# Layer 2's neighbour weights as 32x32 products in half steps, and layer 1 taken chunk by chunk on two banks

## The chip, the cores and the metric

One core of one Trainium2 chip runs the whole program as one launch. The metric is device time in microseconds: the time from the start to the end of an execution, median of several runs. Five engines work side by side, each through its own instruction queue in order, and meet at semaphores: PE (TensorE, matmul, with its weight loads PEld), DVE (VectorE), ACT (ScalarE), POOL (GpSimd) and SP (SyncE, which here only issues DMAs).

## The reference, cut to what matters

Four graph layers follow one another on 2048 nodes with 64 features each, x of 2048x64 and adj of 2048x2048 with entries 0 or 1. After each layer the input is added and the row is normalised.

```python
# layer 0
deg = max(sum(adj, axis=1) + 1, 1)
z = concat([X, (adj @ X + X) / deg]) @ W + b;  out = relu(z) / |relu(z)|
# layer 1
u = tanh([X, t] @ W1 + b1) @ W2 + b2;  XB = X @ B.T
out = u + adj @ XB - sum(adj, axis=1) * XB
# layer 2: weights halve from each neighbour to the one before it
rank = cumsum(adj != 0, axis=1);  deg = rank[:, -1];  k = min(deg, 100)
pos = rank - (deg - k);  w = (adj != 0) * where(pos > 0, 0.5 ** (k - pos), 0)
out = w @ (input @ weight) + bias
# layer 3
s = adj @ (tanh(|x|) * x / |x|);  out = (arctanh(|s|) * s / |s|) @ kernel + bias
```

So four products with a 2048x2048 matrix are made, three with adj and one with w. For a neighbour in w only the number of later neighbours in its row counts: each of them halves its weight.

## The kernel before, in words

The 2048 nodes (columns of the transposed matrix) are cut into 4 chunks `e` of 512 and into 16 blocks `c` of 128. The adjacency comes in 16 loads of 128 rows (`load_lower` on SP, `load_upper` on ACT). DVE turns each load with two 32x32 stream transposes into bf16 (`transposes`, L550 to L557), into `AT[:, c, e]`, 128 partitions by 512 columns per block and chunk. All four layers' sums over neighbours then are 16 matmuls per chunk of 128x128 by 128x512 (`sum_block`, L801), `XP` (x in two fp16 parts) standing and the matrix moving.

Per chunk of layer 0, PE counts each row's neighbours by quarter (`counts`, L845, products with 32 output rows, four of them side by side in the array), ACT copies the counts to `cnt` (`take_counts`, L381), PE makes the degrees from them (`degrees`, L875), and DVE takes these (`take_degrees`). PE sums (L801) and adds the own row (`add_own`), ACT takes the sum (`take_sum`, L391), PE multiplies with the layer's weights (`dense`, L934), POOL scales the own part by the degree (`weigh`, L276), and DVE finishes the chunk: `activate0`, `combine0`, `normalise`, the last of which ends with two instructions (L561, L562) that write the parts XP of layer 1. Layer 1 needs all four chunks' parts for every sum. It also needs `transpose_x` (L827), `take_xt`, `hidden` (L903) and `take_hidden`, each of which uses the one bank psX in turn.

Layer 2's weights are made beside layers 0 and 1. A bf16's bits, read as int16, grow by 128 where the number doubles. So PE forms, in fp32, 12800 where there is a neighbour, less 128 for each later neighbour, and ACT writes it with a Relu as int16 into `WT`, where it is read as the bf16 weight. Before, this is a running sum, the "chain": two sums that stay in two banks, each going down eight blocks of a chunk, 64 blocks in all. A block is two products of 128x128 by 128x512,

```python
nc.tensor.matmul(acc, C("past"), AT[:, c + 1, e], start=False, stop=False, ...)   # L890
nc.tensor.matmul(acc, C("own"), AT[:, c, e], start=False, stop=True, ...)         # L892
```

and one eviction of 128x512 (`take_chain`, L397); block n waits until the eviction of block n-2 has freed its bank. The order of the whole is written out by hand, engine by engine: where the 64 blocks stand among the sums is in `CHAIN_IN_SUMS` and at the end of the PE program (L945 to L1053). 38 of the 64 blocks stand ahead of the last chunk's counts, 8 more up to the last parts of layer 1, and 18 behind.

Line numbers are those of the kernel before; the changed kernel's differ.

## Time and profile before

| | |
|---|---|
| median of 3 runs | 167.0 us (166.5 to 167.3) |
| profiled execution, own time | 167.19 us |
| profiled execution, span of the instructions | 165.3 us |
| busy: PE, PEld | 123.7 us (75%), 67.6 us |
| busy: DVE, ACT, POOL | 105.8 us (64%), 70.6 us, 46.3 us |

The page cuts the span into 40 slices of 4.1 us and gives each engine's busy share in tenths:

```profile
PE   0000269996999999999997999989999899992000
DVE  0164997999999999998961115500623888538861
ACT  0030215477567866715814576721113310257440
PEclk9999999999999999999999999999999999998555
```

The row PEclk is the clock that TensorE was granted, in tenths of its upper level. Rows of a timeline give start and duration in microseconds from the start of the span; `x16` means 16 instructions in one row; `[1.06 <-DVE AT L557]` is idle time of the engine ahead of the row and the instruction that ended it. Products overlap in the array, so the distance of two starts is what a product costs PE, and its duration is how long until its result is there.

### The profile page before, as it was taken

How to read it: one execution, taken by the hardware profiler on the slowest of the kernel's cores; microseconds unless marked ns; L12 is line 12 of the kernel's file. 1: busy time of each engine (PE TensorE's matmuls, PEld its weight loads, DVE VectorE, ACT ScalarE, POOL GpSimd, SP SyncE). 2: the span in 40 equal slices, each digit the busy share in tenths (PEclk: the TensorE clock that was granted, in tenths of full speed). 3: DMA queues.
4: the chain of work that ended last, by engine and by line, in shares of the span. 5: the costliest groups of instructions: out<-in, count | busy, mean ns of one | idle time of the engine just before them, and what ended most of it. 6: DMA issues, size and time to landing. Idle time of an engine off the chain costs nothing.

```text
span 165.3 us, 2143 instructions
## 1 busy us (share of the span) xinstructions
PE 123.7 (75%) x760; PEld 67.6 (41%) x760; DVE 105.8 (64%) x235; ACT 70.6 (43%) x143; POOL 46.3 (28%) x54
## 2 busy tenths in 40 slices
PE   0000269996999999999997999989999899992000
PEld 0000159841444345346344667337447644572000
DVE  0164997999999999998961115500623888538861
ACT  0030215477567866715814576721113310257440
POOL 0000002412401241027931024400412552713290
PEclk9999999999999999999999999999999999998555
DMA  3999999999999940000000000000000000000006
GB/s 110 255 238 357 354 289 252 337 344 340 339 345 346 300 147 0 0 4 0 0 0 0 0 4 0 2 0 4 0 0 0 0 2 0 4 0 0 0 0 127
DMA packets 13946, 18.59 MB, mean 112 GB/s; under 512 B 5360, under 2 KB 5616, under 8 KB 13936
## 3 DMA queue, kind: packets, MB, share of 16 engines
q1 hardware_dynamic: 7728, 9.68, 20.6%
q10 hardware_dynamic: 6208, 8.78, 18.0%
q8 instruction: 6, 0.10, 0.2%
q14 instruction: 4, 0.03, 0.1%
HBM read 17.93 MB, written 0.52 MB: 112 GB/s over the span
## 4 chain that ended last, share of the span: by engine, by line
DVE 34%; PE 34%; DMA 13%; ACT 5%; POOL 4%; issue 4%; SPq 2%; POOLq 1%; DVEq 0%
PE psS L801 11%; DVE AT L556 8%; DMA stage<-adj 7%; DMA WT<-adj 7%; DVE AT L557 6%; PE psN L801 5%; PE psC L801 5%; POOL root L287 2%; PE psC L892 2%; PE psC L890 2%; POOL nroot L306 2%; DVE XP L562 2%; ACT WT L397 2%; DVE XP L561 1%; DVE u L579 1%
## 5 line engine op out<-in xcount | busy, mean ns | idle before, releaser
L397 ACT ACTIVATE WT<-psC 128x512 int16<-128x512 f32 x64 | 36.5, 597 | 13.3 <-PE psC L892 12.4
L801 PE MATMUL psS<-AT,XP 128*128 128x512 bf16 x112 | 29.9, 379 | 1.3 <-DVE XP L562 1.3
L287 POOL TENSOR_TENSOR root<-var,power 128x4 f32<-128x4 f32 (+1 forms) x16 | 18.7, 1172 | 36.5 <-DVE var L603 14.6
L892 PE MATMUL psC<-AT,cb 128*128 128x512 bf16 x64 | 24.2, 379 | 0.0
L890 PE MATMUL psC<-AT,cb 128*128 128x512 bf16 x56 | 21.4, 382 | 1.6 <-ACT WT L397 1.5
L556 DVE STREAM_TRANSPOSE AT<-stage 128x1024 bf16<-128x1024 bf16 x10 | 13.0, 1304 | 10.0 <-DMA stage<-adj 10.0
L801 PEld LDWEIGHTS psS<-AT,XP 128*128 128x128 f16 x112 | 10.4, 98 | 15.1 <-DVE XP L562 2.3
L854 PE MATMUL psH<-AT,cb 128*32 128x256 bf16 x32 | 1.7, 344 | 18.9 <-DVE AT L557 18.9
L300 POOL TENSOR_TENSOR XB<-X,weights 128x256 f32<-128x256 f32 x12 | 10.0, 843 | 18.4 <-DVE X L608 18.4
L557 DVE STREAM_TRANSPOSE AT<-stage 128x1024 bf16<-128x1024 bf16 x10 | 12.7, 1273 | 0.0
L391 ACT ACTIVATE stage<-psS 128x512 f32<-128x512 f32 x6 | 3.6, 596 | 17.6 <-PE psS L801 11.4
L890 PEld LDWEIGHTS psC<-AT,cb 128*128 128x128 bf16 x56 | 5.8, 103 | 12.1 <-ACT WT L397 9.1
L619 DVE TENSOR_TENSOR t<-psH,XB 128x256 f32<-128x256 f32 x3 | 1.3, 425 | 14.1 <-PE psH L937 13.1
L619 DVE TENSOR_TENSOR t<-psN,XB 128x256 f32<-128x256 f32 x3 | 1.3, 424 | 12.8 <-PE psN L937 8.4
L801 PE MATMUL psN<-AT,XP 128*128 128x512 bf16 x32 | 9.2, 379 | 0.0
L608 DVE TENSOR_TENSOR X<-t,root 128x256 f32<-128x256 f32 x16 | 7.3, 479 | 2.9 <-POOL root L287 2.8
L556 DVE STREAM_TRANSPOSE AT<-WT 128x1024 bf16<-128x1024 bf16 x6 | 8.0, 1328 | 1.6 <-DMA WT<-adj 1.6
L854 PEld LDWEIGHTS psH<-AT,cb 128*32 128x32 bf16 x32 | 0.9, 111 | 19.0 <-issue 18.9
L281 POOL TENSOR_TENSOR ssroot<-ss,power 128x4 f32<-128x4 f32 x4 | 4.1, 1023 | 15.5 <-DVE ss L581 15.3
L801 PE MATMUL psC<-AT,XP 128*128 128x512 bf16 x32 | 7.7, 379 | 0.8 <-ACT WT L397 0.8
L412 ACT ACTIVATE v<-t 128x256 f32<-128x256 f32 x12 | 4.9, 421 | 7.7 <-DVE t L619 6.7
L801 PE MATMUL psS<-WT,XP 128*128 128x512 bf16 x32 | 7.9, 379 | 0.0
(156 smaller groups left out, 231.1 us busy)
## 6 DMA issues: line engine op xcount, KB each, us to landing
stage<-adj ACTq DMA_DIRECT2D x20, 256.0 KB, 11.3
stage<-adj SPq DMA_DIRECT2D x20, 256.0 KB, 13.4
WT<-adj ACTq DMA_DIRECT2D x12, 256.0 KB, 12.5
WT<-adj SPq DMA_DIRECT2D x12, 256.0 KB, 16.8
out<-X SPq DMA_DIRECT2D x6, 64.0 KB, 2.0
weights<-weights_packed SPq DMA_DIRECT2D x1, 353.5 KB, 17.2
X<-x SPq DMA_DIRECT2D x2, 128.0 KB, 6.8
X<-x ACTq DMA_DIRECT2D x2, 128.0 KB, 8.2
```

The costliest lines, as they stand in the source:

```text
L281: nc.gpsimd.tensor_tensor(ssroot[:, chunk(e)], ss[:, chunk(e)], power[:, 0, 0:NR], ALU.pow).then_inc(ssroot_ready, 1)
L287: nc.gpsimd.tensor_tensor(root[:, e, 0:n], var[:, e, 0:n], power[:, 0:n, 0:NR], ALU.pow).then_inc(root_ready, 1)
L300: nc.gpsimd.tensor_tensor(XB[:, chunk(e)], X[:, chunk(e)], per_feature(W(f"b{l}")), ALU.add).then_inc(xb_ready, 1)
L391: nc.scalar.activation(to.rearrange("p (k h b) -> p k h b", h=2, b=QD), natural(sum_bank(l, e)[:]), ACT.Copy, scale=scale).then_inc(sum_ta ...
L397: nc.scalar.activation(WT[:, e, chain_block(bank, k)], psC[bank][:], ACT.Relu).then_inc(chain_taken, 1)
L412: nc.scalar.activation(v[:, chunk(e), 0:D], t[:, chunk(e)], ACT.Square, scale=0.125).then_inc(square_ready, 1)
L556: nc.vector.transpose(to[:, :, :, :, 0], halves[:, :, 0, :, :, 1])
L557: nc.vector.transpose(to[:, :, :, :, 1], halves[:, :, 1, :, :, 1]).then_inc(transposed, 1)
L608: nc.vector.tensor_tensor(X[:, chunk(e)], t[:, chunk(e)], per_node(root[:, e, 0]), ALU.mult).then_inc(x_ready, 1)
L801: ins = nc.tensor.matmul(bank, XP[:, l % 2, c], matrix, start=(c == 0), stop=last)
L890: nc.tensor.matmul(acc, C("past"), AT[:, c + 1, e], start=False, stop=False, skip_group_check=True)
L892: nc.tensor.matmul(acc, C("own"), AT[:, c, e], start=False, stop=True, skip_group_check=(k > 0)).then_inc(chain_ready, 1)
```

## The change

**The chain.** The 64 blocks become 16 steps of four blocks. psC is now four banks, one for each quarter (32 partitions of the block). In a step, quarter q of block g gets two products of 32x32 by 32x512: one of the table `base` with `later` (the counts of all later blocks and quarters, so no running sum is left), and one of `own` with 32 partitions of AT. A half step is two quarters: 8 products of the first kind and 8 of the second, in two banks; ACT evicts both banks at once (128x1024). The half step waits until its own two banks are free. `later` comes from a new product (`spread`) and a new eviction (`take_spread`), once per chunk, between the counts and the degrees; degrees now wait for it.

**Order within layer 2.** WT now holds the nodes in another order. So layer 2's parts are written to ZP, turned by 16 products per chunk (`turn`), and evicted to XP (`take_turned`).

**Layer 1.** Its four sums had banks of their own and ran side by side; now they use two (psN, psS), chunk by chunk. The counts of chunks 1 to 3 go to psX, which transpose_x and hidden use too. Of the last chunk, the counts and sums of 384 columns are made as soon as 15 of the 16 transposes are done, the rest after the sixteenth.

**The rest.** The centring of the weights goes from DVE's end of layer 0 to its fourth transpose, `weights` is loaded one load earlier, `activate0` keeps its rows in `v`, and its first instruction is a step of its own (`add_own_part`). POOL forms the residuals of chunks 0 and 1 right after their diagonals.

Around the counts of the last chunk PE had this order before (psX: the bank of transposes and hidden products; L845 are the counts):

```order
L827 MATMUL psX<-cb,XP 128x128 x4
L890 MATMUL psC<-AT,cb 128x512
L892 MATMUL psC<-AT,cb 128x512
L890 MATMUL psC<-AT,cb 128x512
L892 MATMUL psC<-AT,cb 128x512
L903 MATMUL psX<-stage,weights 128x512
L845 MATMUL psH<-AT,cb 32x512 x16
L801 MATMUL psS<-AT,XP 128x512 x8
L875 MATMUL psH<-cb,cnt 128x1 x4
L801 MATMUL psS<-AT,XP 128x512 x8
```

and has this one now (L968 is the dense product, L852 the transpose, L940 hidden, L872 the counts, L915 and L920 a half step):

```order
L968 MATMUL psH<-weights,sum 128x64 x4
L852 MATMUL psX<-cb,XP 128x128 x4
L940 MATMUL psX<-stage,weights 128x512
L852 MATMUL psX<-cb,XP 128x128 x4
L915 MATMUL psC<-later,cb 32x512 x8
L920 MATMUL psC<-AT,cb 32x512 x8
L915 MATMUL psC<-later,cb 32x512 x8
L920 MATMUL psC<-AT,cb 32x512 x8
L940 MATMUL psX<-stage,weights 128x512
L872 MATMUL psX<-AT,cb 32x384 x16
```

Two transposes and two hidden products, where there was one of each, now stand ahead of the last counts, and the counts wait for the second `take_hidden`. ACT's queue at the same place before, from the chain's evictions of chunk 2 to the counts:

```order
L375 ACTIVATE stage<-psX 128x512
L397 ACTIVATE WT<-psC 128x512 x2
L408 ACTIVATE stage<-psX,weights 128x512
L381 ACTIVATE cnt<-psH 128x512
L391 ACTIVATE sum<-psS,xs 128x512
```

and now:

```order
L395 ACTIVATE sum<-psS,xs 128x512
L402 ACTIVATE WT<-psC 128x1024
L375 ACTIVATE stage<-psX 128x512
L418 ACTIVATE stage<-psX,weights 128x512
L375 ACTIVATE stage<-psX 128x512
L402 ACTIVATE WT<-psC 128x1024 x2
L418 ACTIVATE stage<-psX,weights 128x512
L380 ACTIVATE cnt<-psX 128x512
```

Here too a second pair of take_xt (L375) and take_hidden (L418) has come in, and the two evictions of a chain step (L402) stand between them.

The diff, cut to its core:

```diff
-CCOLS = {"ident": P, "paired": P, "own": P, "past": P, "begin0": P, "begin1": P, "count": QD, "each": 1}
+NBLOCKS = 16
+CCOLS = {"ident": P, "paired": P, "own": QD, "base": NBLOCKS * QD, "spread": P, "count": NQ * QD, "each": 1}
...
-        psS = [psum(f"psS{i}", [P, CW], F32) for i in range(2)]
-        psC = [psum(f"psC{i}", [P, CW], F32) for i in range(2)]
-        psN = [psum(f"psN{i}", [P, CW], F32) for i in range(2)]
+        ZP = Z[:].rearrange("p c f -> p (c f)").bitcast(F16).rearrange("p (c f) -> p c f", c=NB)
+
+        psC = psum("psC", [P, NQ, CW], F32)
+        psS = psum("psS", [P, CW], F32)
+        psN = psum("psN", [P, CW], F32)
...
         def sum_bank(l, e):
-            return psS[0] if l == 0 else (psS[1], psN[1], psS[0], psC[0])[e]
+            if l == 0:
+                return psS[:]
+            return (psN[:], psS[:])[e % 2] if l == 1 else (psN[:], psC[:, 2], psC[:, 3], psS[:])[e]
 
         def z_bank(e):
-            return (psN[0], psN[1], psS[1], psC[0])[e]
+            return (psN[:], psC[:, 1], psC[:, 2], psC[:, 3])[e]
 
         def dense_bank(l, e):
-            return psN[0] if l == 0 else (psN[0], psH)[e % 2] if l == 1 else (psN[0], psH, psX, psC[1])[e]
-
-        CHAIN_IN_SUMS = (0, 10, 27, 38)
-        CHAIN_LOOP = 46
-        CHAIN_ALL = NB * NE
-
-        def chain_in_sums(e):
-            return range(CHAIN_IN_SUMS[e], min(CHAIN_IN_SUMS[e] + NB // 2, NB * e))
-
-        def chain_after_sums(e):
-            return range(chain_in_sums(e).stop, CHAIN_IN_SUMS[e + 1])
+            if l == 0:
+                return psH[:]
+            return (psH[:], psH[:], psX[:], psH[:])[e] if l == 1 else (psH[:], psX[:], psC[:, 0], psC[:, 1])[e]
+
+        def turn_bank(e):
+            return psC[:, e % 2]
...
                 diagonals(e)
-            e = NE - 2
-            weigh(e)
-            l2_root(e)
-            weigh(e + 1)
-            residual(1, 0)
-            var_root(0, e)
-            diagonals(e)
-            residual(1, 1)
-            l2_root(e + 1)
-            diagonals(e + 1)
+                residual(1, e)
+            weigh(2)
+            diagonals(2)
+            l2_root(2)
+            weigh(3)
+            l2_root(3)
+            var_root(0, 2)
+            var_root(0, 3)
+            diagonals(3)
...
+            def take_spread(e):
+                act.wait_ge(spread_ready, e + 1)
+                nc.scalar.activation(natural(later[:, e % 2]), psX[:].rearrange("p (k h b) -> p k h b", h=2, b=QD),
+                                     ACT.Copy).then_inc(spread_taken, 1)
...
-            def take_chain(n):
-                act.wait_ge(chain_ready, n + 1)
-                e, k, bank = n // NB, n % NB // 2, n % 2
-                nc.scalar.activation(WT[:, e, chain_block(bank, k)], psC[bank][:], ACT.Relu
+            def take_chain(i, h):
+                act.wait_ge(chain_ready, PAIRS * i + h + 1)
+                e, m = i // NR, i % NR
+                tiles = slice(NQ * m + PAIRS * h, NQ * m + PAIRS * (h + 1))
+                nc.scalar.activation(WT[:, e, tiles], psC[:, PAIRS * h:PAIRS * (h + 1)], ACT.Relu
                                      ).then_inc(chain_taken, 1)
 
-            def take_pair(n):
-                take_chain(n)
-                take_chain(n + 1)
+            def take_step(i):
+                for h in range(PAIRS):
+                    take_chain(i, h)
+
+            def take_turned(e):
+                act.wait_ge(turned, e + 1)
+                nc.scalar.activation(XP[:, 0, chunk(e)], turn_bank(e).rearrange("p (Q f) -> p Q f", Q=NQ),
+                                     ACT.Copy).then_inc(turned_taken, 1)
...
+            take_step(7)
+            take_spread(2)
+            take_chain(8, 0)
+            take_sum(0, 2)
+            take_chain(8, 1)
+            take_xt(1, 0)
+            take_hidden(0)
+            take_xt(1, 1)
+            take_step(9)
+            take_hidden(1)
+            take_counts(3)
+            take_sum(0, 3)
+            take_spread(3)
+            take_step(10)
...
-                parts = XP[:, l % 2, chunk(e)]
+                parts = ZP[:, chunk(e)] if l == 2 else XP[:, l % 2, chunk(e)]
...
             transposes(14)
+            add_own_part(2)
             transposes(15)
             activate0(2)
-            bundle = W(CENTRED[0], CENTRED[-1]).rearrange("p (k f) -> p k f", f=D)
-            step(nc.vector.tensor_reduce(wmean[:], bundle, AX_X, ALU.add))
-            nc.vector.scalar_tensor_tensor(bundle, wmean[:].unsqueeze(2).to_broadcast([P, len(CENTRED), D]), -1.0 / D,
-                                           bundle, ALU.mult, ALU.add).then_inc(centred, 1)
             take_degrees(3)
+            add_own_part(3)
+            activate0(3)
             combine0(2)
-            activate0(3)
+            combine0(3)
             normalise(0, 2)
-            combine0(3)
             normalise(0, 3)
...
+            def counts(e, cols=slice(0, CW)):
+                if e == NE - 1:
+                    pe.wait_ge(hid_taken, 2)
+                bank = psH if e == 0 else psX
...
+            def spread(e):
+                pe.wait_ge(counts_taken, e + 1)
+                nc.tensor.matmul(psX[:], C("spread"), cnt[:].rearrange("p r Q b -> p (r Q b)"), start=True, stop=True
+                                 ).then_inc(spread_ready, 1)
+
             def degrees(e):
-                pe.wait_ge(counts_taken, e + 1)
+                pe.wait_ge(spread_taken, e + 1)
                 for r in range(NR):
                     c = NR * e + r
-                    ins = nc.tensor.matmul(psH[:, c:c + 1], cnt[:, e % 2, r].rearrange("p Q b -> p (Q b)"),
+                    ins = nc.tensor.matmul(psX[:, c:c + 1], cnt[:, r].rearrange("p Q b -> p (Q b)"),
                                            C("each"), start=True, stop=True)
                 ins.then_inc(deg_ready, 1)
 
-            def chain(n):
-                e, k, bank = n // NB, n % NB // 2, n % 2
-                acc, c = psC[bank][:], chain_block(bank, k)
-                if n == 0:
+            def chain(i):
+                e, m = i // NR, i % NR
+                if i == 0:
                     pe.wait_ge(z_taken, NE)
-                if n >= 2:
-                    pe.wait_ge(chain_taken, n - 1)
-                if k == 0:
-                    nc.tensor.matmul(acc, C(f"begin{bank}"), cnt[:, e % 2].rearrange("p r (k h) b -> p (r k) b h", h=2),
-                                     start=True, stop=False)
-                else:
-                    nc.tensor.matmul(acc, C("past"), AT[:, c + 1, e], start=False, stop=False,
-                                     skip_group_check=True)
-                nc.tensor.matmul(acc, C("own"), AT[:, c, e], start=False, stop=True,
-                                 skip_group_check=(k > 0)).then_inc(chain_ready, 1)
-
-            def chain_pair(n):
-                chain(n)
-                chain(n + 1)
+                if m == 0:
+                    pe.wait_ge(spread_taken, e + 1)
+                for h in range(PAIRS):
+                    if i >= 1:
+                        pe.wait_ge(chain_taken, PAIRS * (i - 1) + h + 1)
+                    for q in range(PAIRS * h, PAIRS * (h + 1)):
+                        rows = slice(QD * q, QD * (q + 1))
+                        for g in range(NQ):
+                            c = NQ * m + g
+                            nc.tensor.matmul(psC[QD * g:QD * (g + 1), q], C("base")[rows, QD * c:QD * (c + 1)],
+                                             later[rows, e % 2], start=True, stop=False)
+                    for q in range(PAIRS * h, PAIRS * (h + 1)):
+                        rows = slice(QD * q, QD * (q + 1))
+                        for g in range(NQ):
+                            ins = nc.tensor.matmul(psC[QD * g:QD * (g + 1), q], C("own")[rows],
+                                                   AT[rows, NQ * m + g, e], start=False, stop=True)
+                    ins.then_inc(chain_ready, 1)
+
+            def turn(e):
+                pe.wait_ge(parts_ready, parts_count(2, e))
+                pe.wait_ge(chain_taken, PAIRS * STEPS)
+                if e >= 2:
+                    pe.wait_ge(turned_taken, e - 1)
+                for q in range(NQ):
+                    for g in range(NQ):
+                        ins = nc.tensor.matmul(turn_bank(e)[QD * g:QD * (g + 1), P * q:P * (q + 1)],
+                                               C("ident")[:, QD * q:QD * (q + 1)], ZP[:, NQ * e + g],
+                                               start=True, stop=True)
+                ins.then_inc(turned, 1)
...
+            for e in range(1, NE - 1):
+                pe.wait_ge(transposed, NR * (e + 1))
+                pe.wait_ge(deg_taken, e)
+                counts(e)
+                for c in range(NB):
+                    sum_block(0, e, c)
+                    if c == 1:
+                        chain(NR * e - 1)
+                    if c == 5:
+                        spread(e)
+                    if c == 10:
+                        degrees(e)
+                    if c == 11:
+                        chain(NR * e)
+                add_own(0, e)
+                sums(1, 0, range(e - 1, e))
+                dense(0, e)
...
+            pe.wait_ge(transposed, NB - 1)
+            counts(e, most)
+            pe.wait_ge(sum_taken, e)
+            sum_cols(e, 0, 3)
             pe.wait_ge(transposed, NB)
+            counts(e, rest)
+            sum_cols(e, 3, 4)
+            chain(10)
+            spread(e)
             degrees(e)
+            dense(0, e)
+            sums(1, 1, range(0, 1))
+            chain(11)
+            sums(1, 1, range(1, 2))
+            chain(12)
+            transpose_x(1, 2)
+            sums(1, 0, range(2, 3))
+            hidden(2)
+            sums(1, 1, range(2, 3))
+            chain(13)
             sums(1, 0, late)
             add_own(1, 0)
+            transpose_x(1, 3)
             sums(1, 1, late)
             add_own(1, 1)
+            hidden(3)
             dense(1, 0)
+            chain(14)
+            sums(1, 2, every)
             add_own(1, 2)
             dense(1, 1)
+            chain(15)
+            sums(1, 3, every)
+            add_own(1, 3)
             dense(1, 2)
+            turn(0)
+            turn(1)
             dense(1, 3)
+            for g in range(2):
+                for e in every:
+                    sums(2, e, range(g, g + 1))
+            turn(2)
+            turn(3)
```

## Rows read from the trace of the kernel before

**Rows 1.** Windows, us from the start of the span: busy time of each engine and granted clock.
```profile
core 0: us, PE busy (x) PEld busy (x) DVE busy (x) ACT busy (x) POOL busy (x), PEclk, DMA share, GB/s
...
69.90:87.70 17.80, 16.55 (x99) 7.93 (x100) 15.32 (x35) 7.26 (x13) 10.14 (x11) 1.00 0.00 1
87.70:112.10 24.40, 23.18 (x140) 13.47 (x141) 5.28 (x12) 14.29 (x28) 4.72 (x5) 1.00 0.00 1
...
149.80:151.90 2.10, 0.02 (x1) 0.00 (x0) 1.83 (x10) 1.13 (x6) 0.00 (x0) 1.00 0.00 0
151.90:165.30 13.40, 0.00 (x0) 0.00 (x0) 7.54 (x30) 5.00 (x22) 5.64 (x5) 0.50 0.19 39
```

**Rows 2.** Timeline of PE, 41 to 57 us: start, duration, instructions, [idle before <-releaser].
```profile
41.38 1.05 PE L845 MATMUL psH<-AT,cb 128*32 128x512 bf16 x16 [1.06 <-DVE AT L557]
42.35 0.61 PE L801 MATMUL psS<-AT,XP 128*128 128x512 bf16 x2
...
56.98 1.05 PE L845 MATMUL psH<-AT,cb 128*32 128x512 bf16 x16
```

**Rows 3.** Groups of instructions on ACT: count, busy us, mean ns, idle before.
```profile
L397 ACT ACTIVATE WT<-psC 128x512 int16<-128x512 f32 x64 | 36.5, 597 | 13.3 <-PE psC L892 12.4
...
L364 ACT ACTIVATE Z<-psN 128x256 f32<-128x256 f32 x2 | 0.8, 384 | 0.4 <-PE psN L836 0.4
```

**Rows 4.** Timeline of ACT: one pair of the chain's evictions.
```profile
37.23 1.09 ACT L397 ACTIVATE WT<-psC 128x512 int16<-128x512 f32 x2 [0.21 <-PE psC L892]
```

**Rows 5.** Timeline of DVE, chunk 0 of layer 0, 36 to 47 us.
```profile
36.60 0.29 DVE L578 TENSOR_SCALAR y<-t 128x256 f32<-128x256 f32 x1
...
38.83 1.33 DVE L556 STREAM_TRANSPOSE AT<-WT 128x1024 bf16<-128x1024 bf16 x1
...
41.23 0.38 DVE L589 TENSOR_TENSOR t<-y,ssroot 128x256 f32<-128x256 f32 x1
...
43.09 1.31 DVE L556 STREAM_TRANSPOSE AT<-stage 128x1024 bf16<-128x1024 bf16 x1
...
45.48 0.38 DVE L608 TENSOR_TENSOR X<-t,root 128x256 f32<-128x256 f32 x1
...
46.22 0.43 DVE L562 SCALAR_TENSOR_TENSOR XP<-X,XP 128x256 f16<-128x256 f32 x1
46.56 1.32 DVE L556 STREAM_TRANSPOSE AT<-stage 128x1024 bf16<-128x1024 bf16 x1
```

**Rows 6.** Timeline of DVE, chunk 3 of layer 0, 73 to 88 us.
```profile
73.58 0.15 DVE L568 TENSOR_SCALAR degp<-psH 128x4 f32<-128x4 f32 x1
...
77.06 0.42 DVE L576 TENSOR_TENSOR t<-psN,Z 128x256 f32<-128x256 f32 x1 [0.32 <-PE psN L934]
...
86.77 0.83 DVE L562 SCALAR_TENSOR_TENSOR XP<-X,XP 128x256 f16<-128x256 f32 x1
```

**Rows 7.** Timeline of POOL, 74 to 88 us.
```profile
74.21 0.72 POOL L276 TENSOR_TENSOR Z<-Z,degp 128x256 f32<-128x256 f32 x1 [1.56 <-DVE ndeg L570]
...
86.49 0.83 POOL L300 TENSOR_TENSOR XB<-X,weights 128x256 f32<-128x256 f32 x1 [0.54 <-DVE X L608]
```

**Rows 8.** Timeline of PE, 69 to 121 us.
```profile
69.89 1.05 PE L845 MATMUL psH<-AT,cb 128*32 128x512 bf16 x16 [0.36 <-DVE AT L557]
...
79.60 1.02 PE L903 MATMUL psX<-stage,weights 128*128 128x512 f32 x2
80.46 0.38 PE L890 MATMUL psC<-AT,cb 128*128 128x512 bf16 x1
...
92.33 0.33 PE L936 MATMUL psN<-weights,stage 128*128 128x64 f32 x2
...
94.06 0.38 PE L890 MATMUL psC<-AT,cb 128*128 128x512 bf16 x1
...
120.74 1.89 PE L801 MATMUL psS<-WT,XP 128*128 128x512 bf16 x8
```

358 lines of the change are left out of this document (154 added, 204 removed).

## The prediction, made before the changed kernel was run

> **What bounds the kernel now.** I read the page's slices first, then windows, then the timelines of PE, ACT, DVE and POOL from 40 to 132 us. The slices show two regimes: to about 70 us DVE is full (the 16 transposes and layer 0 between them), from there PE is, until 150. The windows say the same in numbers: after the last chunk's counts begin, PE is busy 16.55 of 17.80 us, then 23.18 of 24.40 [rows 1]. Between the two lies one path: the counts of the last chunk start at 69.89 [rows 8], DVE takes the degrees at 73.58, the dense product at 77.06, and writes layer 1's last parts up to 86.77 + 0.83 = 87.60 [rows 6]. In those 17.8 us PE lives on blocks of the chain. Whoever makes the chain cheap frees PE, but the path has to become shorter too, or PE waits.
>
> The profiled execution took 167.19 us for a span of 165.3; the median of the runs is 167.0. I work out a shift of the span and add it to 167.0. Less than 0.5% (0.84 us) can't be told from no change.
>
> **Prices.** Eight sums of 512 columns last 1.89 us, the last one 0.38 of it, so one costs PE (1.89 - 0.38)/7 = 0.216, and its result comes 0.17 later [rows 8]. The 16 products of the counts, four at a time in the array, cost 42.35 - 41.38 = 0.97 us [rows 2]: four rounds of 0.216, and 0.10 for the change of tiling. So column tiles run fully side by side. No row shows row tiles. If they did nothing, a step's 32 products would be 8 rounds, 1.73 us, as much as the eight products of four blocks now (8 x 0.216). If all 16 tiles ran freely it would be 2 rounds, 0.43. I take 3 rounds, since the second product of a half must wait for the first on its own tiles while the next half can start beside it: 0.65, and with two changes of tiling 0.85. I take it nearer the fast end, because the nearest row, the counts, shows no loss at all from sharing the array.
>
> The page "TensorE: Matmul & The Clock Gate" of the Trainium skill (Measured speedup vs the span model) gives 10.6x for 16 tiles of 32x32. That lies near the fast end; no row here shows it, and by it a step would be some 0.2 us shorter than mine.
>
> An eviction of 512 columns takes 597 ns, one of 256 takes 384 [rows 3], so 1024 columns are 597 + 512 x 0.83 = 1.02 us. A second one behind the first costs 1.09 - 0.60 = 0.49 [rows 4], so one of 1024 costs 0.49 + 0.43 = 0.92. ACT then needs 1.84 us a step; now it spends 1.09 + 0.21 on a pair of blocks, 2.6 on four [rows 4]. On ACT the chain falls from 64 x 0.49 = 31 us to 16 x 1.84 = 29, with 8 new evictions of 0.6: nothing won.
>
> **The change up to the last chunk's counts.** Taken from PE here: 38 blocks of 0.43; added: 10 steps of 0.85. None of it shows while DVE is full. DVE pays a little: residual(1, 0) now runs on POOL while DVE writes chunk 0's parts, and one DVE instruction beside such a POOL instruction takes 0.83 [rows 6, 7] against 0.43 [rows 5], so 0.4. The centring (1.2 us) falls into DVE's wait for the fifth load, which I book at 0.3, with `weights` ahead of a load; between 0 and 1. So the counts of chunk 2 start at 56.98 + 0.7 = 57.7 [rows 2].
>
> From there everything stands in one line, since psX is passed from hand to hand. Chunk 2: counts 0.97, 16 sums 3.45, spread, degrees and own row 0.55, steps 7 and 8 1.7, result 0.2: 64.6. take_sum 0.6 and dense 0.85 (16 fp32 products cost 94.06 - 92.33 = 1.73, eight of them half [rows 8]): 66.1. Transpose 0.4, eviction 0.6, hidden 0.86 + 0.17 (80.46 - 79.60 [rows 8]), eviction 0.6: 68.7. Transpose 0.4 and eviction 0.6: 69.7. The second hidden product is made under step 9, but ACT has the step's two evictions in front of take_hidden, 1.9 + 0.6: 72.2. Only then is psX free for the last counts. Before, they started at 69.89, as soon as DVE was done; that early start of three quarters of them, which the change provides, is lost in this queue.
>
> **From the counts to layer 1's last parts.** Counts and sums of 384 columns 0.75 + 2.6 + 0.2; the rest 0.3 + 0.1 + 0.9 + 0.1; step 10 0.85; spread 0.4, its eviction 0.6, degrees 0.3: 7.1, so 79.3, against 73.58 [rows 6]. DVE has stood still since 73 and holds combine0(2) behind take_degrees(3). Then degrees 0.5, weigh 0.7 [rows 7], the own part 0.4, activate0 38.83 - 36.60 = 2.2, two combine0 of 43.09 - 41.23 = 1.86, normalise(0, 2) 46.56 - 45.48 = 1.1 [rows 5]: 87.9. normalise(0, 3) 1.1 + 0.4 (a diagonal on POOL beside it): 89.4, against 87.6. PE runs out of work at about 84.5 and waits until 87.9.
>
> **Layer 1 and the start of layer 2.** From 87.9: transpose, 8 sums, hidden, step 13: 3.6. Then 8 sums 1.7, own rows 0.4, transpose and hidden 1.1, waits for take_hidden(2) and take_xt, which stand behind evictions of step 13, 1.1. Four dense products 6.9, steps 14 and 15 1.7, 32 sums 6.9, own rows 0.4, two turns 0.6 (16 products of 128 columns are four rounds of 0.056). That ends at 112.3. Half of layer 2's sums 6.9: 119.2. The last two turns and the wait for their eviction (0.1 + 0.22 + 0.2 + 0.6 + 0.1): 120.4, or 120.7 with a DVE step of `activate0` now writing rows of 65 elements (up to 0.13 four times). Before, the same sums start at 120.74 [rows 8]. From here nothing changes but banks, 0 to 0.2. So PE's saving (26 blocks of 0.43 = 11 us less 6 steps of 0.85 = 5) is eaten by the later parts, 1.8, by 20 more sums behind them, 4.3, less what lies ahead of the last parts, by turns of 1.5 and by waits. The waits for ACT in layer 1 and DVE's cost ahead of chunk 2 are unsure by 0.4 each, and the bounds put both on top: shift 0 to +0.8, taken as +0.4: **167.4 us**.
>
> **Rivals.**
>
> *The path is shorter than I reckon (faster).* If the hand-overs on psX overlap more, or ACT reaches take_hidden(1) ahead of step 9's evictions, the last counts start with DVE's end, 2.5 us earlier, and with them the parts. PE has the spare time for it: it stands 3.4 us in my account. 167.4 - 2.5 = 164.9, down to 162 if DVE never waits. For it speaks the 6 us less of work on PE, and that a stage whose engine is full at 93% gains from less work; against it, that each link of the path has a row of its own.
>
> *The clock falls (slower).* PE's clock stayed full from 25.6 to 149.8 us, in which its longest pause was 1.06 us [rows 2], and was at 0.50 from 151.9, 2.1 us after its last product [rows 1]. The change brings pauses: about 3 us ahead of chunk 1's counts, 3.5 ahead of chunk 2's, 3.4 before 87.9. If the clock is at 1.2 GHz after one of them, PE-bound work runs at half speed until it comes back; at the start it took from 21.9 to 25.6, so 3.7 us at half speed, 1.85 lost. The place is 87.9 us, where every us counts: 169.3; with a second fall at 57.7, 171.1. It decides as soon as a pause of 2 us or more comes in mid-kernel. Against it: the one fall seen came after a stretch of fp32 products, and a pause in mid-kernel of this length is in no row.
>
> The same page of the Trainium skill (HAM oscillation) warns of just this, pauses between bursts of products that bring the clock back down; the only pause of that kind in this trace, the end, agrees with it.
>
> *Row tiles don't run side by side (slower; the change then doesn't do what it says).* A step costs 1.08 more. Of the 16, steps 7, 8, 10, 13, 14 and 15 lie on my path: +6.5, less 1 that ACT's pace hides: 173.
>
> **Chances.** My own account, within 1.2 us of 167.4: 0.38, of which 0.22 is no change and 0.16 slower. Faster by the shorter path: 0.30. The clock: 0.22. Row tiles: 0.10. Faster 0.30, same 0.22, slower 0.48. The range takes in the clock's double fall and leaves out row tiles and the lowest of the fast cases: 164.3 to 171.1.
>
> **What would show it.** Right: starts of L915 and L920 within a half in groups of eight, a step's first start to the next PE instruction 0.75 to 0.95; last counts (L872, 32x384) at 71 to 73; a DVE pause of 5 us or more ended by degrees; a PE pause of 3 us before the transpose of chunk 2; layer 2's third group of sums at 120 to 122. Wrong: the last counts ahead of 70, or PE without a pause between 80 and 88 (then faster); groups of four (row tiles); a PEclk under 1.00 between 26 and 150 us.

## The result and the profile after

| | before | after |
|---|---|---|
| median | 167.0 us (166.5 to 167.3, 4 runs) | 173.4 us (172.8 to 173.9, 4 runs) |
| ratio | | 1.038, 95% interval 1.034 to 1.043 |
| span of the profiled execution, its own time | 165.3, 167.19 us | 172.0, 173.86 us |
| busy: PE, PEld | 123.7, 67.6 us | 113.2, 63.2 us |
| busy: DVE, ACT, POOL | 105.8, 70.6, 46.3 us | 106.2, 70.5, 46.2 us |

The change made the kernel 3.8% slower, and the time lies above my range of 164.3 to 171.1. PE's busy time is 10.5 us lower and the span 6.7 us longer. (The trace of the changed kernel has lost some records of products: the page counts 1230 beside 1244 weight loads. Run 1 below has them all; less its 52 extra products of 0.216 us its busy time is 110.5 us, so at full clock PE does 13 us less than before.) The slices of the changed kernel:

```profile
PE   0000289970986499669735979999989989994000
...
PEclk9999999995699569999995799999999999999555
```

Two things are new. PE has holes in the slices that begin at 38.7, 55.9 and 86.0 us (each is 4.3 us). And PEclk is low in three places in mid-kernel, where before it was full. The windows of the changed kernel give the clock its bounds (columns as in [rows 1]):

```profile
core 0: us, PE busy (x) PEld busy (x) DVE busy (x) ACT busy (x) POOL busy (x), PEclk, DMA share, GB/s
...
39.10:45.90 6.80, 2.88 (x37) 0.80 (x50) 6.56 (x13) 1.98 (x3) 2.40 (x3) 0.50 1.06 340
45.90:56.20 10.30, 8.33 (x162) 3.65 (x131) 9.96 (x19) 7.59 (x9) 2.90 (x4) 1.00 1.06 339
56.20:63.00 6.80, 4.31 (x61) 0.96 (x53) 6.66 (x10) 2.39 (x4) 2.26 (x3) 0.50 0.67 194
...
90.30:97.10 6.80, 4.79 (x13) 2.11 (x14) 4.51 (x9) 0.60 (x1) 3.75 (x5) 0.50 0.00 0
```

At 0.50 the clock is at the lower of its two levels, 1.2 instead of 2.4 GHz ("half clock" below). PE's timeline shows what it did before each fall. The longest idle time in mid-kernel before the change was 1.06 us [rows 2]:

```profile
35.19 0.41 PE L915 MATMUL psC<-later,cb 32*32 32x512 bf16 x8
...
37.93 0.41 PE L915 MATMUL psC<-later,cb 32*32 32x512 bf16 x8 [0.29 <-ACT WT L402]
38.15 0.40 PE L920 MATMUL psC<-AT,cb 32*32 32x512 bf16 x8
42.69 1.90 PE L872 MATMUL psX<-AT,cb 128*32 128x512 bf16 x16 [4.14 <-DVE AT L573]
```

```profile
54.88 0.41 PE L915 MATMUL psC<-later,cb 32*32 32x512 bf16 x8 [1.10 <-ACT WT L402]
...
56.02 0.53 PE L920 MATMUL psC<-AT,cb 32*32 32x512 bf16 x8
58.71 1.90 PE L872 MATMUL psX<-AT,cb 128*32 128x512 bf16 x16 [2.16 <-DVE AT L573]
```

```profile
87.72 0.40 PE L920 MATMUL psC<-AT,cb 32*32 32x512 bf16 x8
92.31 0.58 PE L852 MATMUL psX<-cb,XP 128*128 128x128 bf16 x4 [4.19 <-DVE XP L578]
```

The first fall, at 39.1, came 0.55 us after PE's last product, and ahead of that PE had made a half step every 0.92 us. The second, at 56.2, came in the half step at 56.02, after a pause of 1.10; the pause of 2.16 came only then. The third, at 90.3, came some 2.2 us into a pause of 4.19. The 16 counts then took 1.90 us, against 1.05 at full clock [rows 2, 8].

The milestones of the path, in the order of the prediction (start of the PE row, where no other is named; the last column is the run with extra products that follows):

| | before | predicted | after | after, clock kept full |
|---|---|---|---|---|
| counts, chunk 1 | 41.38 | | 42.69 | 42.65 |
| counts, chunk 2 | 56.98 | 57.7 | 58.71 | 57.90 |
| counts, chunk 3 | 69.89 | 72.2 | 75.96 | 73.44 |
| DVE takes its degrees | 73.58 | 79.3 | 83.17 | 80.65 |
| PE goes on with chunk 2's parts | | 87.9 | 92.31 | 89.79 |
| last parts written (DVE) | 87.60 | 89.4 | 95.12 | 92.61 |
| layer 2, third group of sums | 120.74 | 120.4 to 120.7 | 127.68 (see below) | 122.67 |

The row at 127.68 holds 7 of the 8 products of its group, so the group will have started one product earlier, at about 127.46. From the third group on both kernels take the same, 44.6 and 44.5 us to the end of the span. DVE's timeline around the last chunk shows the other half of the loss, the wait for the degrees, with work for chunk 2 standing behind them:

```profile
75.17 0.43 DVE L603 SCALAR_TENSOR_TENSOR v<-ymean,v 128x256 f32<-128x256 f32 x1
83.17 0.16 DVE L584 TENSOR_SCALAR degp<-psX 128x4 f32<-128x4 f32 x1 [7.58 <-PE psX L898]
...
91.73 0.43 DVE L578 SCALAR_TENSOR_TENSOR XP<-X,XP 128x256 f16<-128x256 f32 x1
92.27 1.26 DVE L627 TENSOR_TENSOR X<-t,root 128x256 f32<-128x256 f32 x1
...
94.29 0.83 DVE L578 SCALAR_TENSOR_TENSOR XP<-X,XP 128x256 f16<-128x256 f32 x1
```

And PE's, ahead of the last counts, the hand-overs on psX. For the idle 0.82 us the profile names no releaser; `transpose_x(1, 1)` waits there for the first `take_hidden`, which runs on ACT from 71.50 to 72.19:

```profile
69.27 0.39 PE L852 MATMUL psX<-cb,XP 128*128 128x128 bf16 x4
70.34 1.12 PE L940 MATMUL psX<-stage,weights 128*128 128x512 f32 x2 [0.69 <-ACT stage L375]
72.29 0.38 PE L852 MATMUL psX<-cb,XP 128*128 128x128 bf16 x4 [0.82 <-issue]
...
73.36 1.12 PE L940 MATMUL psX<-stage,weights 128*128 128x512 f32 x2
75.96 0.83 PE L872 MATMUL psX<-AT,cb 128*32 128x384 bf16 x16 [1.47 <-ACT stage L418]
```

### The profile page after: what moved, and what is told of

It is laid out like the page before. It is cut to its first block, busy times and chain, and to the rows that moved or that the text cites. A ratio compares the mean times of both kernels' runs of the same rounds, so it can differ in the third digit from the quotient of the medians.

```text
span 172.0 us, 3082 instructions
## 1 busy us (share of the span) xinstructions
PE 113.2 (66%) x1230; PEld 63.2 (37%) x1244; DVE 106.2 (62%) x235; ACT 70.5 (41%) x119; POOL 46.2 (27%) x54
## 4 chain that ended last, share of the span: by engine, by line
PE 37%; DVE 29%; DMA 10%; ACT 8%; issue 4%; POOL 4%; SPq 4%; POOLq 1%; another core or an unknown queue 0%; DVEq 0%
DMA stage<-adj 10%; PE psN L823 7%; PE psC L823 7%; PE psS L823 6%; DVE AT L573 6%; DVE AT L572 6%; ACT WT L402 3%; PE psX L940 2%; PE psS L880 2%; SPq L246 2%; POOL nroot L308 2%; PE psX L872 2%; PE psH L970 2%; PE psH L971 2%; POOL root L289 2%
## 5 line engine op out<-in xcount | busy, mean ns | idle before, releaser
L402 ACT ACTIVATE WT<-psC 128x1024 int16<-128x1024 f32 x32 | 31.1, 1022 | 15.5 <-PE psC L920 14.8
L823 PE MATMUL psS<-AT,XP 128*128 128x512 bf16 x74 | 20.5, 397 | 1.2 <-issue 1.1
L872 PE MATMUL psH<-AT,cb 128*32 128x256 bf16 x32 | 1.7, 343 | 19.1 <-DVE AT L573 19.1
L823 PEld LDWEIGHTS psS<-AT,XP 128*128 128x128 f16 x80 | 7.4, 102 | 12.8 <-issue 6.3
L915 PE MATMUL psC<-later,cb 32*32 32x512 bf16 x256 | 9.2, 409 | 2.7 <-ACT WT L402 2.7
L627 DVE TENSOR_TENSOR X<-t,root 128x256 f32<-128x256 f32 x16 | 8.1, 534 | 4.1 <-POOL root L289 4.0
L872 PE MATMUL psX<-AT,cb 128*32 128x512 bf16 (+2 forms) x64 | 5.0, 451 | 7.8 <-DVE AT L573 6.3
L880 PE MATMUL psS<-AT,XP 128*128 128x256 bf16 (+2 forms) x64 | 9.3, 304 | 0.2 <-ACT cnt L380 0.2
L920 PE MATMUL psC<-AT,cb 32*32 32x512 bf16 x256 | 9.0, 394 | 0.0
L852 PE MATMUL psX<-cb,XP 128*128 128x128 bf16 x32 | 3.5, 240 | 7.5 <-DVE XP L578 4.2
L872 PEld LDWEIGHTS psH<-AT,cb 128*32 128x32 bf16 x32 | 0.9, 111 | 19.2 <-issue 19.1
L572 DVE STREAM_TRANSPOSE AT<-WT 128x1024 bf16<-128x1024 bf16 x6 | 7.9, 1312 | 0.0
L573 DVE STREAM_TRANSPOSE AT<-WT 128x1024 bf16<-128x1024 bf16 x6 | 7.7, 1279 | 0.0
L823 PE MATMUL psC<-WT,XP 128*128 128x512 bf16 x32 | 7.6, 379 | 0.0
```

Of the source, the lines that this page charges most:

```text
L402: nc.scalar.activation(WT[:, e, tiles], psC[:, PAIRS * h:PAIRS * (h + 1)], ACT.Relu).then_inc(chain_taken, 1)
L572: nc.vector.transpose(to[:, :, :, :, 0], halves[:, :, 0, :, :, 1])
L573: nc.vector.transpose(to[:, :, :, :, 1], halves[:, :, 1, :, :, 1]).then_inc(transposed, 1)
L627: nc.vector.tensor_tensor(X[:, chunk(e)], t[:, chunk(e)], per_node(root[:, e, 0]), ALU.mult).then_inc(x_ready, 1)
L823: ins = nc.tensor.matmul(sum_bank(l, e), XP[:, l % 2, c], matrix, start=(c == 0), stop=last)
L872: ins = nc.tensor.matmul(bank[QD * g:QD * (g + 1), cols], one, AT[:, NQ * g + k, e, cols], start=(k == 0), stop=(k == NR - 1))
```

## The experiments

The kernel before ran beside each group of runs, at 166.9 to 167.1 us. Theory at this point: of the 6.4 us, the clock's three falls are some 4 and the path to layer 1's parts the rest. The rival: the falls cost nothing, since they lie in pauses, and all is path. Where milestones of two runs are compared below, note that the loads alone move them: chunk 2's counts start at 58.13 us in run 8 and at 57.24 in run 11, which differ only behind them.

**1. The clock kept full.** Products whose result nobody reads fill PE's pauses; the kernel's own waits stay, and one is added so that the bank of the last group is free. 52 of them, of 512 columns, stand around steps 1 and 2, 5 and 6, and 12:

```diff
+            def keep_busy(bank, n):
+                for _ in range(n):
+                    nc.tensor.matmul(bank, C("ident"), AT[:, 0, 0], start=True, stop=True)
...
+            keep_busy(psN[:], 1)
             chain(1)
+            keep_busy(psN[:], 1)
             chain(2)
+            keep_busy(psN[:], 17)
...
                     chain(NR * e + 1)
+                    keep_busy(psS[:], 4)
                     chain(NR * e + 2)
+                    keep_busy(psS[:], 8)
...
+            pe.wait_ge(dense_taken, NE)
+            keep_busy(psH[:], 4)
             chain(12)
+            keep_busy(psH[:], 17)
```

> The changed kernel with extra products of 128x128 by 128x512 on PE, whose results nobody reads, in the three places where its clock fell: between and behind chain steps 1 and 2 (19), behind steps 5 and 6 (12), around step 12 (21). Theory A (the clock is what I missed): PEclk stays 1.00 in all three places; the 1.9 us that chunk 2 of layer 0 took longer at the lower clock and the 2.5 us of the stretch behind 92.3 us come back: 169.0 us, 168.2 to 170. Theory B (the path through the counts and DVE is what costs, the clock falls where PE waits anyway): within 1 us of 173.4.

Measured: 169.4 us (169.0 to 169.7), ratio to before 1.0146 (1.012 to 1.018). The page's row of the clock is full up to the end, and the last counts start at 73.44:

```profile
PEclk9999999999999999999999999999999999999655
```

```profile
38.88 3.84 PE L981 MATMUL psN<-AT,cb 128*128 128x512 bf16 x17
42.65 1.05 PE L872 MATMUL psX<-AT,cb 128*32 128x512 bf16 x16
```

```profile
73.44 0.83 PE L872 MATMUL psX<-AT,cb 128*32 128x384 bf16 x16 [1.47 <-ACT stage L418]
...
89.79 0.38 PE L852 MATMUL psX<-cb,XP 128*128 128x128 bf16 x4 [0.42 <-DVE XP L578]
```

PE has more to do and the kernel is 4.0 us faster. (Chunk 1's counts stand behind the 17 products, 38.88 + 3.84, so they gain nothing here.) So the three falls cost 4.0 us, though each begins in or beside a pause: what costs is that the half clock reaches into the work behind it. The two traces say where: of the changed kernel's delay 0.8 us stand at chunk 2's counts, 1.7 more at the last counts, none up to chunk 2's parts, and 2.3 between these and layer 2's third group (4.8; the two profiled executions themselves differ by 4.9, 173.86 and 169.0). The rest, 169.4 against 167.0, is path.

**2. Only the last fall prevented** (the seven lines around step 12 alone: 4 products, 17 products and the wait).

> The same extra products around step 12 alone, so the clock falls only twice. Theory A: the third fall costs 2.5 us, all of it on the path: 170.9 us, and the first two falls stay where they were. Theory B: within 0.7 us of 173.4.

Measured: 171.5 us (169.9 to 172.3), ratio 1.025 (1.018 to 1.033). Two early stretches at half clock stayed (38.3 to 48.6 and 58.8 to 62.2), none late. So by the medians the late one is worth some 1.9 us, the early two together 2.1; the runs spread over 2.4 us, so the split is unsure by about 1. The traces above gave 2.3 and 2.5.

**3. DVE's order around the last degrees.** Chunk 2 is finished before the last degrees are awaited, as it was not in the change:

```diff
             activate0(2)
+            combine0(2)
+            normalise(0, 2)
             take_degrees(3)
             add_own_part(3)
             activate0(3)
-            combine0(2)
             combine0(3)
-            normalise(0, 2)
             normalise(0, 3)
```

and on POOL `var_root(0, 2)` stands ahead of `weigh(3)`.

> The changed kernel with combine0(2) and normalise(0, 2) ahead of take_degrees(3) on DVE (and chunk 2's root ahead of weigh(3) on POOL), in DVE's pause of 7.6 us. If DVE's queue behind the degrees is on the path: 3.0 us less, and since the transpose, hidden product and sums of chunk 2 then fill PE's pause before 92 us, the third fall of the clock should go as well: 168 us, 167 to 169.5. If only the last counts' own time matters (PE-bound behind it): 1 us or less.

Measured: 167.7 us (167.3 to 168.4, 10 runs), ratio 1.005 (1.003 to 1.007). DVE's wait for the degrees shrank from 7.58 us to 2.77, and chunk 2's transpose on PE had no pause ahead of it, so the third stretch at half clock was gone as well:

```profile
79.57 0.42 DVE L578 SCALAR_TENSOR_TENSOR XP<-X,XP 128x256 f16<-128x256 f32 x1
82.76 0.16 DVE L584 TENSOR_SCALAR degp<-psX 128x4 f32<-128x4 f32 x1 [2.77 <-PE psX L898]
```

```profile
87.71 0.40 PE L852 MATMUL psX<-cb,XP 128*128 128x128 bf16 x4
...
93.14 1.04 PE L823 MATMUL psN<-AT,XP 128*128 128x512 bf16 x4 [1.04 <-DVE XP L578]
```

This one order is worth 5.7 us, the largest single part. By run 2 some 1.9 of it is the third fall. Against run 2 itself, where the late clock is full as well, it is 3.8 us, but not all of that is the wait for the degrees: the last counts, ahead of everything the order touches, start at 75.62 here and at 76.12 in run 2, with the early stretches at half clock shorter (6.8 and 3.4 us, against 10.2 and 3.4). That leaves some 3.3 for the wait itself.

**4. The centring put back** behind DVE's last transposes, with the residuals of chunks 0 and 1 behind `l2_root(2)` on POOL and the load of the weights one load later:

```diff
+            transposes(4)
+            transposes(5)
             dve.wait_ge(weights_loaded, 16)
...
-            bundle = W(CENTRED[0], CENTRED[-1]).rearrange("p (k f) -> p k f", f=D)
...
-            transposes(4)
-            transposes(5)
             take_degrees(0)
...
             activate0(2)
+            bundle = W(CENTRED[0], CENTRED[-1]).rearrange("p (k f) -> p k f", f=D)
...
             take_degrees(3)
```

> The changed kernel with the centring back behind activate0(2), the load of the weights back behind the fourth load, and residual(1, 0) and (1, 1) on POOL behind l2_root(2). If DVE's early part is what moved the first two chunks: counts of chunk 1 at 41.4 instead of 42.7, of chunk 2 at 57.0 instead of 58.7, and 1.7 us less: 171.7 us. If the later waits absorb it: within 0.7 us of 173.4.

Measured: 172.5 us (172.0 to 172.9), ratio 1.033 (1.030 to 1.036): 0.9 us, between the two. Chunk 1's counts start at 42.39, 0.3 earlier, and chunk 2's at 58.73, no earlier than in the change. DVE waits for chunk 0's degrees, which in the profiled execution of the change were there without a wait:

```profile
32.92 0.17 DVE L720 SCALAR_TENSOR_TENSOR weights<-weights 128x1 f32<-128x1 f32 x1
34.34 0.16 DVE L585 TENSOR_SCALAR degp<-psX 128x4 f32<-128x4 f32 x1 [1.25 <-PE psX L899]
```

The degrees stand behind `spread` and its eviction now: from chunk 0's second counts to the degrees PE takes 2.85 us here (31.20 to 34.05), 1.62 in the kernel before. That wait is not the centring's doing alone. With the centring early, as in the change, DVE still waited 1.26, 0.63 and 1.11 us in runs 2, 3 and 5, and took the degrees at 34.73, 34.49 and 34.38, against 34.34 here: wherever the centring stands, they come at the same time. As in run 3, though, the second stretch at half clock was 3.4 us long and the last counts start 0.4 earlier (75.57), near half of the 0.9.

**5. Second transpose and hidden product behind the last counts**, so that only one pair passes psX ahead of them:

```diff
                     transpose_x(1, 0)
                     hidden(0)
-                    transpose_x(1, 1)
                     chain(NR * e + 1)
-                    hidden(1)
...
             chain(11)
+            transpose_x(1, 1)
             sums(1, 1, range(1, 2))
+            hidden(1)
             chain(12)
```

with ACT's `take_xt(1, 1)` and `take_hidden(1)` behind step 11.

> The changed kernel with transpose_x(1, 1), hidden(1) and their two evictions behind the last chunk's degrees, between steps 11 and 12, so that the last counts wait for the first take_hidden alone. Theory A (the hand-over of psX in front of the last counts is on the path): the last counts start near 73 instead of 75.96 us and 3 us go: 170.4 us, 169.5 to 171.3. Theory B (what is moved comes back behind the parts, where PE is full): within 0.8 us of 173.4.

Its four runs gave 169.1 us three times and 166.4 once, and only one of the 169.1 was profiled. So this run gives no firm size: the gain is 4.3 us by three of the runs and 7.0 by the fourth, of which no trace exists. In the trace that there is, the last counts start at 71.98 instead of 75.96 and the pause before chunk 2's parts shrank to 2.60 us, and the third stretch at half clock with it (88.9 to 92.4); with the second stretch, 3.4 us here too, that is why it is more than expected.

**6. The chain at near its old price.** Every half step makes its 16 products twice.

```diff
                 for h in range(PAIRS):
                     if i >= 1:
                         pe.wait_ge(chain_taken, PAIRS * (i - 1) + h + 1)
+                    for _ in range(2):
...
```

> The changed kernel with the 16 products of every half step made twice, so that a step costs PE 8 rounds, as much as the four blocks before; nothing else changes. It asks what the cheap chain is worth in this order. If PE's work counts where the steps lie on the path (7, 8, 10, 13 to 15): 5 us more, 178. If the chain was hidden and the clock is what matters, less pausing pays back: 171 to 174.

Measured: 178.4 us (177.6 to 180.1), ratio 1.065 (1.061 to 1.069). The last counts start at 79.19. So the cheap products do shorten the path, by 5.0 us in this order, although the denser PE also had less of the half clock (13.7 us in three stretches, against 20.5 in the change). And since the doubled kernel stands 11.4 us above the kernel before, what surrounds the products, the clock's falls with it, loses at least that much. A doubled step is still cheaper than four blocks were: two quarters' second pass runs beside the other half's first. PE's rows of run 10, which has the same steps, show it:

```profile
62.21 0.41 PE L917 MATMUL psC<-later,cb 32*32 32x512 bf16 x8
62.44 0.40 PE L922 MATMUL psC<-AT,cb 32*32 32x512 bf16 x8
62.62 0.44 PE L917 MATMUL psC<-later,cb 32*32 32x512 bf16 x16
62.84 0.44 PE L922 MATMUL psC<-AT,cb 32*32 32x512 bf16 x16
63.05 0.44 PE L917 MATMUL psC<-later,cb 32*32 32x512 bf16 x8
63.27 0.46 PE L922 MATMUL psC<-AT,cb 32*32 32x512 bf16 x8
63.66 1.04 PE L824 MATMUL psS<-AT,XP 128*128 128x512 bf16 x4
```

It takes 63.66 - 62.21 = 1.45 us, a single step at this place 0.61 (below), four blocks before 1.73.

**7. The three orders together** (runs 3, 4 and 5).

> DVE's order of e3_dve_order, the centring back as in e4_centring_back, and the late hidden product of e6_hidden_late together. If the three act on the same path one after the other: 167.7 less 3 less 0.9, so 163.8 us, 162.5 to 165.5, faster than the kernel before (167.0). If PE is full behind the last parts by then and only the front moves: 166 to 167.5.

Measured: 166.4 us (165.4 to 167.5, 12 runs), ratio 0.997 (0.994 to 0.999). The second reading holds; the gains are not a sum. The clock was still at half from 40.0 to 46.8 and from 57.1 to 63.9.

**8. The same with the first two places filled** (18 products around steps 1 and 2, 12 around steps 5 and 6; none late, since no pause is left there).

> The same with the extra products of e1_warm_all behind chunks 0 and 1 (18 and 12), not around step 12. By the clock theory the two falls before 60 us go and 1.5 to 2 us with them against e8_all_orders: 162 us. If DVE's queue sets the pace there: within 0.5 us of e8_all_orders.

Measured: 164.1 us (163.6 to 164.6, 6 runs), ratio 0.982 (0.979 to 0.985). It is 2.9 us below the kernel before. PEclk is full from start to end of the products:

```profile
PEclk9999999999999999999999999999999999999555
```

**9. Run 8 with the centring where the change put it.**

> As the run with all three orders and the early extra products (164.1 us), but the centring and the residuals stand where the change put them. Putting them back was worth 0.9 us in the changed kernel as it is. Theory A (what precedes chunk 2's counts is on the path, whatever the clock): slower by about 0.9, so 165.0. Rival (the 0.9 came with the places of the clock's falls, which are gone here): 164.1 within 0.3.

Measured: 164.1 us (163.3 to 164.6), ratio 0.983 (0.978 to 0.987). The rival holds: in run 8 DVE waited 1.31 us for chunk 0's degrees, here it does the centring in that time, and the counts of chunk 2 start at 57.94, against 58.13. The centring's place is worth nothing by itself.

**10. Run 8 with the chain doubled, as in run 6.**

> As the run with all three orders and the early extra products (164.1 us), with each half step's 16 products made twice, so that a block costs PE about what it cost before the change. It asks what the cheap products are worth where neither the clock nor the queues cost anything. In the changed kernel doubling cost 5.0 us. Theory A (PE's work from chunk 2's counts on lies on the path; ten of the 16 steps are made behind chunk 2's counts, 0.43 us more each): +4 to +5, so 168 to 169, above the kernel before. Rival (with the queues in order DVE sets the end of layer 0, and only the six steps behind it count): +2.5, so 166.6.

Measured: 172.7 us (172.0 to 173.4), ratio 1.034 (1.030 to 1.039). That is 8.6 us above run 8; both theories were too low. Chunk 2's counts start 2.6 us later (60.70 against 58.13), the last counts 4.3 (74.38 against 70.04), the third group of layer 2's sums 8.1 (126.24 against 118.14). My expectation took 0.43 us for a second pass, and ten steps behind chunk 2's counts. There are nine (7 to 15), and a second pass costs 1.45 - 0.61 = 0.84 us; so they bring up to 7.6, and most of PE's work there is on the path (8.1 - 2.6 = 5.5). Of the 2.6 ahead of it some are loads: DVE waited for them for 1.90, 0.55 and 1.16 us, against 1.14 and 0.28 in run 8. Why they came later was not tried. This run has nearly the old price of the chain, the clock full and the queues in order, and is still 5.6 us above the kernel before. What of this is due to spread, to the turning, to layer 1 on two banks or to the rest, no run separates.

**11. Run 8 with both hidden products ahead of the last counts, as in the change.**

> As the run with all three orders and the early extra products (164.1 us), but the second transpose and hidden product stand ahead of the last chunk's counts, as in the change. Theory A (psX's hand-over is on the path to the last counts): last counts near 72 instead of 70.04, time 165 to 166. Rival (with the clock full the hand-over fits beside DVE's work): 164.1 within 0.3.

Measured: 164.9 us (164.3 to 166.1, 7 runs), ratio 0.988 (0.984 to 0.992). In between: the last counts start at 72.79, 2.75 us later than in run 8 (3.6 counted from chunk 2's counts, 57.24 and 58.13), and the time grows by 0.75. DVE shows why. In run 8 it reaches the degrees at 79.70, as soon as chunk 2's parts are written, though PE had made them at 76.90; here it waits for them:

```profile
79.36 0.42 DVE L579 SCALAR_TENSOR_TENSOR XP<-X,XP 128x256 f16<-128x256 f32 x1
79.70 0.15 DVE L585 TENSOR_SCALAR degp<-psX 128x4 f32<-128x4 f32 x1
```

```profile
78.43 0.42 DVE L579 SCALAR_TENSOR_TENSOR XP<-X,XP 128x256 f16<-128x256 f32 x1
79.93 0.16 DVE L585 TENSOR_SCALAR degp<-psX 128x4 f32<-128x4 f32 x1 [1.08 <-PE psX L899]
```

With chunk 2 finished first, DVE's work covers most of the hand-over on psX. In the change nothing covered it: DVE only waited there, and in run 5's trace it takes the degrees as much earlier (79.20 against 83.17) as the counts start earlier.

## Why the prediction was wrong

**The clock: the step that failed first.** I named it as a rival, gave it 0.22, at most two falls of 1.85 us and a top of 171.1. There were three, 4.0 us together (run 1). The reasoning against it was "the one fall seen came after a stretch of fp32 products, and a pause in mid-kernel of this length is in no row". That a pause of 2 us is in no row before was no evidence that it is harmless, when the change brings three of them and the only long pause shown [rows 1] ended at half clock. Of the three pauses I foretold, "about 3 us ahead of chunk 1's counts, 3.5 ahead of chunk 2's, 3.4 before 87.9", the profile shows 4.14, 2.16 and 4.19. The condition, "as soon as a pause of 2 us or more comes", was too mild: two of the falls came earlier than that, in or just after half steps with short pauses between them. The one price, 1.85, was near for the late place (1.9 by run 2, 2.3 by the traces) and too high for the early ones (2.1 to 2.5 for two). By the Trainium skill, "TensorE: Matmul & The Clock Gate" (HAM oscillation), pauses between bursts bring the clock down; this trace agrees plainly in the third fall, 2.2 us into a pause of 4.19. The first came 0.55 us into one, and the second between half steps, where the longest pause had been 1.10.

**The path to the last counts.** From chunk 2's counts I reckoned 57.7 to 72.2, 14.5 us. With the clock kept full it took 15.5 (57.90 to 73.44). The mechanism, psX passed from hand to hand, was right; the terms were too small. Up to take_sum 7.2 us instead of 6.9, although the two steps in it were cheaper than booked: PE stood ahead of the degrees (62.73 in run 1, 0.38 idle <-ACT later L385) until ACT had made spread's eviction, which it reaches only behind both evictions of step 7, a wait that my sum did not have. Then take_sum and dense 1.7 instead of 1.5. And from the dense product's end to the last counts, 6.1 in my sum, it took 6.7, in the changed kernel 6.8. Two hand-overs in the rows above show it: an idle 0.69 [<-ACT stage L375], where I had taken 0.6 for the eviction alone, and 0.82 ahead of the second transpose, for a take_hidden (L418) of 0.69 that I had taken at 0.6.

**DVE ahead of chunk 2's counts.** Booked 0.7, measured 1.7 with the falls (58.71 against 56.98) and 0.9 without (57.90); runs with the same front differ by as much as 0.9. The 0.4 for an instruction of DVE beside a residual is right: 0.83 us in place of 0.43. The centring, booked at 0.3, brought nothing to the time (run 9): where it is not done, DVE waits for chunk 0's degrees instead, made late by `spread`, which I had not priced there.

**From the counts to layer 1's last parts.** 7.1 us from the counts to the degrees on DVE: 7.2 measured. Then 8.6 until PE goes on with chunk 2's parts: 9.1 measured. "DVE has stood still since 73 and holds combine0(2) behind take_degrees(3)" was seen and priced, and is the largest single loss (run 3); my error was to let PE's saving pay for it. The pause of PE at that place was longer than the 3.4 us I took.

**Layer 1 to layer 2's third group.** 87.9 to 120.4 or 120.7, 32.5 to 32.8 us: with the clock kept full 89.79 to 122.67, 32.9. Right.

**The price of a step.** I took 3 rounds, 0.65 us, and 0.85 with the tiling. It is 2 rounds:

```profile
33.41 0.46 PE L915 MATMUL psC<-later,cb 32*32 32x512 bf16 x16
33.63 0.45 PE L920 MATMUL psC<-AT,cb 32*32 32x512 bf16 x16
34.15 1.10 PE L968 MATMUL psH<-weights,sum 128*128 128x64 f32 x8
```

The 16 products of each kind start together, the two kinds 0.22 apart. So all 16 tiles of 32x32 ran at once, and the rival that row tiles are not concurrent is refuted. The changes of tiling, which I had put at 0.2, cost 0.31 ahead of the dense product, which follows 0.74 after the step's first start, 0.31 beyond the 0.43. Ahead of sums they cost 0.18, as here in run 8:

```profile
59.65 0.46 PE L916 MATMUL psC<-later,cb 32*32 32x512 bf16 x16
59.87 0.45 PE L921 MATMUL psC<-AT,cb 32*32 32x512 bf16 x16
60.26 1.04 PE L824 MATMUL psS<-AT,XP 128*128 128x512 bf16 x4
```

So a step costs 0.61 or 0.74 us, not 0.85: this term was too high, in the path's favour, and the path came out longer all the same. By the Trainium skill, "TensorE: Matmul & The Clock Gate" (Measured speedup vs the span model), 16 such tiles give 10.6x. The trace agrees that they run side by side; its own figure is lower, 0.46 us from the first start to the last end, against 15 x 0.216 + 0.38 = 3.62 one after the other, 7.9x. I had written that by 10.6x a step would be 0.2 us shorter than mine. That does not follow: 32 products of 0.216 are 6.9 us, and 6.9 / 10.6, an estimate, is 0.65, the very three rounds that I took. ACT's 1.02 us for 1024 columns was exact (mean 1022 ns, L402), and where ACT sets the pace a half step came every 0.92 us (37.01, 37.93), as computed.

**What adds up.** With the clock kept full the third group starts at 122.67, 2.0 to 2.3 behind my 120.4 to 120.7: 0.2 ahead of chunk 2's counts, 1.0 on psX and around it, 0.1 up to DVE's degrees, 0.5 on DVE, 0.1 to 0.4 behind. The time, 169.4, is 2.0 above my 167.4, but that this fits to a tenth is luck: the 0.4 that I had put on top for the bounds, and the 0.4 by which the median lies above the profiled execution (169.0), cancel. The other 4.0 are the clock.

**Right, against the forecasts named:** groups of eight, a DVE pause of over 5 us ended by degrees, a PE pause before chunk 2's transpose. Wrong: the last counts at 75.96, behind 71 to 73 (73.44 even at full clock), a step's first start to the next product at 0.61 to 0.74, under 0.75 to 0.95, the third group at about 127.5, outside 120 to 122, and PEclk under 1.00 between 26 and 150 us, which I had named as what would refute my account. It did.

## What to carry to other kernels

Work taken off an engine that is not the bound becomes idle time, and on TensorE idle time can be charged twice: here 13 us less work cost 4.0 us through a clock at half speed. Before making TensorE's work sparser, list the pauses that come and either fill them with products nobody reads (30 of them, 6.5 us of PE, won 2.3 us in run 8) or move real work there. And when one engine's saving is to shorten a path, look at the in-order queue that the path runs through: two lines moved on DVE were worth 5.7 us, some 3.3 of them without the clock's part, and with queues and clock in order the same cheap products were worth 8.6 us instead of 5.0 (runs 10 and 6; in run 6 less time at half clock hid a part of their price).

## What the runs showed of the hardware

The clock fell while PE was not fully idle: 16 products of 32x32, in two rounds, every 0.92 us, and 0.55 us after the last of them it was at half (first fall); the kernel before, with pauses of up to 1.06 us between denser work, kept it. It stayed at half for 6.8 us each time in the changed kernel, and for between 3.4 and 10.2 us in the other runs. While it was low in the first stretch, PE was busy 2.88 of 6.8 us.

In a step the products do not start in the order of the queue. The eight L920 of the first half stand there ahead of the eight L915 of the second, on other rows of the array; all 16 L915 start from 33.41 on, and the first L920, which needs the tiles of the first half, at 33.63. And 16 products of 32x32 by 512 columns took 0.22 us of PE, as much as one of 128x128.

A gap in a row can be a lost record and no wait. In the changed kernel's trace, idle times of 0.16 us without a releaser stand ahead of sums that follow a step (66.51, 98.40); these rows hold 3 products where the program has 4, and run 1's rows at the same places (63.76, 93.39) have 4 and no gap.

On DVE, L627 took 1.26 us where POOL's diagonal and residual ran beside it, against 0.42 alone.
